# Another step table for the attention stage: value turns, second unit copy and softmax steps placed at other quarters

## The chip, the cores and the metric

The kernel runs on one core of one Trainium2 chip. The metric is the device time of one execution in microseconds (us), lower is better. A core has TensorE (matmuls and transposes, PE in the profile; its weight loads are PEld), VectorE (DVE), ScalarE (ACT), GpSimd (POOL) and SyncE (SP), which here only issues DMAs. Each engine runs its own instructions in program order; they wait for one another by semaphores.

## The reference, cut to what matters

```python
def _L0_attn_ref(x, Wq, bq, Wk, bk, Wv, bv, Wo, bo):      # x: layer-normed, (4, 512, 1024)
    q = (x @ Wq.T + bq).reshape(B, S, H, D)               # H = 32 heads, D = 32
    k = (x @ Wk.T + bk).reshape(B, S, H, D)
    v = (x @ Wv.T + bv).reshape(B, S, H, D)
    scores = jnp.einsum('bshd,bsgd->bshg', q, k) * inv_sqrt_d     # per token: heads against heads
    scores = jnp.where(scores > THRESH, scores, -jnp.inf)
    attn = jax.nn.softmax(scores, axis=-1)
    out = jnp.einsum('bshg,bsgd->bshd', attn, v).reshape(B, S, Hd)
    return out @ Wo.T + bo

xn = _layernorm(x)
out = x + _L0_attn_ref(xn, ...) + _L0_ffn_ref(xn, ...)    # ffn: int4 weights with group scales, silu(gate) * up, down
```

The attention is over the 32 heads of one token, not over tokens, so each token's scores are a 32 x 32 matrix.

## The kernel before, in words

The 2048 tokens are 16 tiles of 128. The first part of the program turns and splits the weights and projects tile 0. Then `tile_2(i)` is run for i = 1 to 16 (13 of these passes, i = 2 to 14, are a hardware loop). After that come the rest of the output projection and the feed-forward part, 28 tiles of the inner dimension, which the change does not touch.

One pass of `tile_2(i)` has 24 quarters (s = 0 to 23). In each quarter TensorE issues six 128x512 matmuls of the projection of tile i (`project`, L499); four quarters make one "unit", 512 of the 3072 columns of Q, K and V. Units 0 and 1 are Q, 2 and 3 are K, 4 and 5 are V. Behind the matmuls of a quarter stand the steps that the table `STEPS` lists for it. The last pass, i = 16, has no projection: there the quarters hold the turning of Wo (`wo_part`, L567 on TensorE) and the output projection (L586).

The names in `STEPS`, and what each engine does for one:

- **S0 to S3**: scores of the tile before, j = i - 1 (TensorE L529); ScalarE copies them out (L784, four instructions a step).
- **X**: the layer-normed tile i + 1 is split into two f16 parts, ScalarE L756 and VectorE L975.
- **T4 to T7**: the values of tile j, as f16 parts in `stacks`, are turned by TensorE (L513), eight 128x128 transposes a batch. ScalarE copies the even batches to `turned` (L774), VectorE the odd ones (L999). **R0 to R3** are the same for the queries of tile i. Batches use two banks in turn, so a batch waits until the one two before it is copied out (`batch_out`).
- **V0 to V3**: probabilities times values (TensorE L546), copied out by ScalarE (L807) and VectorE (L1028).

Beside the table, at s % 4 == 3, a finished unit is copied: VectorE adds the bias (`unit_copy`, L992), ScalarE makes the two high f16 parts (`unit_part`, L768), GpSimd the two low ones (L1174). R0 waits for the low parts of unit 1. The bank of a unit is free for the next but one when VectorE has copied it.

The softmax of tile j is placed by constants: `SHIFT_AT` (VectorE: row maximum L1006, subtraction L1010), `EXP_AT` (ScalarE: an activation table load and the exponential, L790), `MASK_AT` (VectorE: threshold mask L1014, row sum L1017), `DIVIDE_AT` (VectorE: reciprocal L1021, division L1023), and `P_AT`, where ScalarE writes the high parts of the probabilities (`prob_hi`, L798, eight instructions, the first waits for `norm_done`, the division) and GpSimd the low ones (L1174). SyncE turns them by DMA; V0 waits for the first of four such transposes. SyncE also turns the keys of tile i by DMA; the next pass's S0 waits for it.

In one quarter VectorE does the unit copy first, then the steps of the table, then the softmax piece; ScalarE does the steps of the table, then the softmax piece, then the unit part. So the table and the constants fix the order on each engine:

```python
STEPS = [["S0"], ["S1"], ["S2"], ["S3"], ["X", "T4"], ["T5"], ["T6"], ["T7"], [], [], [], [], ["R0"], ["R1"],
         ["R2"], ["R3"], [], ["V0"], ["V1"], ["V2"], ["V3"], [], [], []]
```

Of the kernel before, what the change touches and what calls it, by code (L numbers as in the profile page):

```python
# [41 lines left out]
def build(nc, x_in, Wq, bq, Wk, bk, Wv, bv, Wo, bo, gate_q, gate_s, up_q, up_s, down_q, down_s, out):  # L42
# [26 lines left out]
    with ExitStack() as whole:  # L69
# [144 lines left out]
        def anchor(eng):  # L214
# [10 lines left out]

        STEPS = [["S0"], ["S1"], ["S2"], ["S3"], ["X", "T4"], ["T5"], ["T6"], ["T7"], [], [], [], [], ["R0"], ["R1"],
                 ["R2"], ["R3"], [], ["V0"], ["V1"], ["V2"], ["V3"], [], [], []]
        QUARTERS = len(STEPS)  # L230

        STATS_AT, ROOT_AT, NORM_AT, SHIFT_AT, EXP_AT, MASK_AT, DIVIDE_AT, P_AT = 0, 2, 2, 3, 4, 5, 6, 8

        LAST_UNITS = (QUARTERS - 2) // 2

# [29 lines left out]
        def steps_of(i, s):  # L265

            for name in STEPS[s]:
                kind, n = name[0], int(name[1:] or 0)
# [1233 lines left out]
```

How the kernel before makes its waits and increments, by code:

```python
        def wait_pos(eng, s, value):  # L292
            if not isinstance(value, int) or value > 0:
                eng.wait_ge(s, value)
# [175 lines left out]
        @block.tensor  # L471
        def _(pe):
            mm, turn = nc.tensor.matmul, nc.tensor.transpose
            pe.wait_ge(const_ready, 2)
            def weights(w):
                pe.wait_ge(w_loaded[w % 4], rows_landed(w))
                wait_pos(pe, w_hi, w - 2)
                wait_pos(pe, w_lo, w - 2)
                for k in range(KT):
                    last = turn(weight_pair(w)[:, k * P:(k + 1) * P], w_rows[:, w % 4, k * P:(k + 1) * P],
                                ident32[:])
                last.then_inc(w_turned, 1)
# [2 lines left out]
            def project(i, s):  # L488
                u, ks = s // 4, range(2 * (s % 4), 2 * (s % 4) + 2)
                if s == 0:
                    pe.wait_ge(x_turned, i * 16 + 16)
                if s % 4 == 0:
                    wait_pos(pe, unit_copied, i * 6 + (u - 1))
# [9 lines left out]
            def batch(j, m):  # L505
                mat = batch_matrix(m)
                if m % 4 == 0:
                    pe.wait_ge(unit_lo, j * 6 + (2 * mat + 2))
                wait_pos(pe, batch_out[m % 2], j * 4 + m // 2)
                for n in range(8):
                    last = turn(batch_bank(m)[:, n * P:(n + 1) * P], stacks[:, mat, 8 * (m % 4) + n, :], ident16[:])
                last.then_inc(batch_done, 1)
# [165 lines left out]
            pe.wait_ge(proj_out, 4 * KT)
            pe.wait_ge(ctx_lo, TT * 4)
```

## Time and profile before

| what | value |
|---|---|
| time, median of 3 runs | 2158.32 us (2156.68 to 2159.87) |
| time of the profiled execution | 2158.44 us |
| its span in the trace | 2156.5 us |
| PE busy | 2034.0 us (94%) |
| DVE busy | 1581.5 us (73%) |
| ACT busy | 1253.2 us (58%) |
| POOL busy | 1348.5 us (63%) |

The difference between the execution's own time and its span lies around the span. Busy shares are means over parts of the program with different limits. The attention passes take the stretch from 78 to about 800 us; the feed-forward part, some 1350 us, comes behind them.

### The profile page before, as it was taken

Reading aid. Unit: us, or ns where it says so; the run is one execution under the profiler, and the core shown is the slowest. Engines: PE = TensorE matmul, PEld = TensorE weight load, DVE = VectorE, ACT = ScalarE, POOL = GpSimd, SP = SyncE. Lnnn points to the kernel's source line nnn. Section 1 sums busy time; section 2 is a strip of 40 time slices with the busy share of each in tenths; the row PEclk is TensorE's granted clock in tenths of the full one; section 3 lists DMA queues with packets and bytes.
Section 4 is the critical chain, followed back from the end, with each engine's and each line's share of the span. In section 5 each row is a group of like instructions: output and inputs, shape, how many; then the busy total and the mean of one; then the engine's idle time right before and its main releaser. Section 6 shows DMA issues by size and latency. Waiting matters only on the chain. (4 is left out here: it accounts for less than half of the span.)

```text
span 2156.5 us, 36938 instructions
## 1 busy us (share of the span) xinstructions
PE 2034.0 (94%) x10880; PEld 973.1 (45%) x10880; DVE 1581.5 (73%) x1584; ACT 1253.2 (58%) x2017; POOL 1348.5 (63%) x769
## 2 busy tenths in 40 slices
PE   8899899989999899989999999999999999999996
PEld 5454445544554444424444444444444444444444
DVE  5565656565656420099999999899989998999897
ACT  4577666766676531226566665666566656565653
POOL 1344454445444200018888888888888888888886
PEclk9999999999999999999999999999999999999998
DMA  8354345444533536211122122112211221122118
GB/s 289 86 118 94 88 93 118 90 88 94 120 88 69 147 93 235 59 44 50 49 66 55 49 58 62 51 49 68 59 44 49 68 58 44 49 68 58 44 25 317
DMA packets 330006, 185.97 MB, mean 86 GB/s; under 512 B 269168, under 2 KB 306032, under 8 KB 329968
## 3 DMA queue, kind: packets, MB, share of 16 engines
q1 hardware_dynamic: 329968, 185.46, 33.0%
q8 instruction: 24, 0.39, 0.1%
q14 instruction: 14, 0.11, 0.0%
HBM read 96.29 MB, written 25.17 MB: 56 GB/s over the span
## 5 line engine op out<-in xcount | busy, mean ns | idle before, releaser
L644 PE MATMUL banks<-xt,lower 128*128 128x512 f16 x3584 | 861.7, 379 | 29.9 <-ACT lower L895 16.2
L1212 POOL TENSOR_TENSOR acc<-acc,lower 128x1024 f32<-128x1024 f32 x327 | 772.0, 2366 | 175.2 <-ACT lower L922 175.2
L922 ACT ACTIVATE lower<-banks,down_scale 128x512 f32<-128x512 f32 x654 | 413.8, 683 | 355.2 <-PE banks L669 263.6
L1099 DVE SCALAR_TENSOR_TENSOR lower<-banks,gate_scale,lower 128x1024 f32<-128x1024 f32 x392 | 479.2, 1277 | 146.2 <-PE banks L644 140.3
L644 PEld LDWEIGHTS banks<-xt,lower 128*128 128x128 f16 x3584 | 337.4, 98 | 486.5 <-DVE lower L1099 80.2
L499 PE MATMUL banks<-wt,xt_tile 128*128 128x512 f16 x2304 | 548.5, 383 | 4.2 <-ACT wt L743 2.6
L1099 DVE SCALAR_TENSOR_TENSOR lower<-banks,up_scale,lower 128x1024 f32<-128x1024 f32 x392 | 479.5, 1278 | 51.0 <-PE banks L644 44.9
L1174 POOL TENSOR_TENSOR stacks<-unit,stacks 128x512 f16<-128x512 f32 x192 | 247.0, 1307 | 375.9 <-ACT stacks L768 375.9
L669 PE MATMUL banks<-lower 128*128 (+1 forms) x1792 | 458.6, 380 | 4.6 <-DMA lower<-lower 4.4
L499 PEld LDWEIGHTS banks<-wt,xt_tile 128*128 (+1 forms) x2304 | 216.7, 99 | 220.1 <-issue 9.9
L669 PEld LDWEIGHTS banks<-lower 128*128 (+1 forms) x1792 | 175.4, 98 | 216.9 <-issue 17.1
L1218 POOL TENSOR_TENSOR lower<-lower 128x1024 f32<-128x1024 f32 x54 | 127.5, 2361 | 191.0 <-DVE lower L1099 191.0
L768 ACT ACTIVATE stacks<-unit 128x512 f16<-128x512 f32 x192 | 110.1, 621 | 131.6 <-DVE unit L992 128.8
L586 PE MATMUL banks<-lower 128*128 128x512 f16 x768 | 170.5, 382 | 3.4 <-ACT acc L820 2.6
L1028 DVE TENSOR_TENSOR ctx_parts<-banks,ctx_parts 32x256 f16<-32x256 f32 x256 | 107.4, 420 | 83.8 <-ACT ctx_parts L807 80.7
L1121 DVE SCALAR_TENSOR_TENSOR acc<-banks,down_scale,acc 128x1024 f32<-128x1024 f32 x106 | 135.6, 1279 | 22.3 <-PE banks L669 22.3
L999 DVE COPY turned<-banks 128x1024 f16<-128x1024 f16 x64 | 77.9, 1217 | 64.4 <-PE banks L513 64.4
L513 PE MATMUL banks<-ident,stacks 128*128 128x128 f16 x1024 | 80.3, 223 | 45.4 <-ACT turned L774 27.7
L807 ACT ACTIVATE ctx_parts<-banks 32x256 f16<-32x256 f32 x256 | 96.0, 375 | 45.1 <-PE banks L546 40.9
L1222 POOL TENSOR_TENSOR lower<-lower 128x1024 f32 (+1 forms) x54 | 115.5, 2139 | 2.1 <-ACT lower L909 2.1
L586 PEld LDWEIGHTS banks<-lower 128*128 128x128 f16 x768 | 74.8, 98 | 92.8 <-issue 6.5
L513 PEld LDWEIGHTS banks<-ident,stacks 128*128 128x128 f16 x1024 | 66.3, 100 | 86.9 <-ACT turned L774 34.8
(57 smaller groups left out, 1331.4 us busy)
## 6 DMA issues: line engine op xcount, KB each, us to landing
lower<-in_L_ffn_gate_q_dram SPq DMA_DIRECT2D x28, 512.0 KB, 3.6
lower<-in_L_ffn_up_q_dram SPq DMA_DIRECT2D x28, 512.0 KB, 4.4
lower<-in_L_ffn_down_q_dram SPq DMA_DIRECT2D x28, 512.0 KB, 3.9
x_tile<-in_L_attn_x_dram SPq DMA_DIRECT2D x16, 512.0 KB, 3.6
xt_scratch<-xt_tile SPq DMA_DIRECT2D x16, 512.0 KB, 2.8
ctx_scratch<-ctx_parts SPq DMA_DIRECT2D x64, 128.0 KB, 2.1
lower<-ctx_scratch SPq DMA_DIRECT2D x4, 2048.0 KB, 9.3
xt<-xt_scratch SPq DMA_DIRECT2D x4, 2048.0 KB, 15.6
```

Of the source, the lines that this page charges most:

```text
L499: last = mm(psum[:, u % 2, :], xt_tile[:, :, :].rearrange("p a b -> p (a b)")[:, bass.ds(at, P)], wt[:, u // 2, wp, k, (u % 2) * BANK:(u % ...
L513: last = turn(batch_bank(m)[:, n * P:(n + 1) * P], stacks[:, mat, 8 * (m % 4) + n, :], ident16[:])
L586: last = mm(psum[:, output_bank(n), :], wo_t[:, wp, k, ho * P:(ho + 1) * P], ctx_t[c % 2][:, :, cp, k, :], start=(k == 0 and m == 0), stop ...
L644: last = mm(psum[:, 2 * (slot % 3) + c, :], gu_t[:, mat, g, :], xt[:, (2 * half + c) * CT:(2 * half + c + 1) * CT, part, g, :], start=(par ...
L669: last = mm(psum[:, bank, :], weights[:, bass.ds((t % 2) * (KT * P) + ho * P, P)], h_flat[:, bass.ds(at, BANK)], start=(part == HI), stop= ...
L922: run(down_tmp[:, buffer, c * BANK:(c + 1) * BANK], psum[:, 6 + c, :], ACT.Copy, scale=scale)\
L1099: v.scalar_tensor_tensor(out=acc_of[:, half, :], in0=gu_pair(slot % 3), scalar=scale[:, :, :].rearrange("p t k -> p (t k)")[:, bass.ds(t * ...
L1121: v.scalar_tensor_tensor(out=acc[:, half, ho, :], in0=gu_pair(slot % 3), scalar=down_scale[:, :, :].rearrange("p h t -> p (h t)")[:, bass. ...
L1174: return g.tensor_tensor(dst, src, hi, ALU.subtract)
L1212: g.tensor_tensor(acc[:, half, ho, :], acc[:, half, ho, :], down_tmp[:, buffer, :], ALU.add).then_inc(down_added, 1)
L1218: g.tensor_tensor(h_sb[:, half, :], h_sb[:, half, :], u_acc[:, half, :], ALU.mult).then_inc(h_done, 1)
L1222: g.tensor_tensor(h_part(t, half, LO), h_sb[:, half, :], h_part(t, half, HI), ALU.subtract)\
```

## The change

The table and four of the eight constants are changed; nothing else is.

```diff
-        STEPS = [["S0"], ["S1"], ["S2"], ["S3"], ["X", "T4"], ["T5"], ["T6"], ["T7"], [], [], [], [], ["R0"], ["R1"],
-                 ["R2"], ["R3"], [], ["V0"], ["V1"], ["V2"], ["V3"], [], [], []]
+        STEPS = [["S0"], ["S1"], ["S2"], ["S3"], ["X"], ["T4"], ["T5"], [], ["T6"], [], ["T7"], [], ["R0"], ["R1"],
+                 ["R2"], ["R3"], ["V0"], ["V1"], [], ["V2"], ["V3"], [], [], []]
-        STATS_AT, ROOT_AT, NORM_AT, SHIFT_AT, EXP_AT, MASK_AT, DIVIDE_AT, P_AT = 0, 2, 2, 3, 4, 5, 6, 8
+        STATS_AT, ROOT_AT, NORM_AT, SHIFT_AT, EXP_AT, MASK_AT, DIVIDE_AT, P_AT = 0, 2, 2, 3, 5, 7, 7, 8
```

On ScalarE, in each pass, this is the piece behind the exponential. L774 is the copy of batch T6, L768 the high parts of unit 1, L798 the high parts of the probabilities.

```order
 L790 ACT_TABLE_LOAD
 L790 ACTIVATE p_c<-p_c 128x1024
-L774 ACTIVATE turned<-banks 128x128x8
-L768 ACTIVATE stacks<-unit 128x16x32 x2
+L768 ACTIVATE stacks<-unit 128x16x32 x2
+L774 ACTIVATE turned<-banks 128x128x8
 L798 ACTIVATE p_stack<-p_c 128x8x32 x8
 L768 ACTIVATE stacks<-unit 128x16x32 x2
```

The copy of T6 and the high parts of unit 1 have changed places; both still stand ahead of the probabilities.

On VectorE, in each pass, this is the piece behind the split of the next tile (L975). The first L999 is the copy of T5, the second that of T7; the first L992 of either order is the copy of unit 1.

```order
 L975 TENSOR_TENSOR x_parts<-x_tile,x_parts 128x1024
 L999 COPY turned<-banks 128x128x8
-L1014 SCALAR_TENSOR_TENSOR p_c<-s_c,p_c 128x1024
-L1017 TENSOR_REDUCE sums<-p_c 128x32
-L1021 RECIPROCAL sums<-sums 128x32
-L1023 TENSOR_TENSOR p_c<-p_c,sums 128x1024
-L992 SCALAR_TENSOR_TENSOR unit<-banks,bias_qkv 128x512
+L992 SCALAR_TENSOR_TENSOR unit<-banks,bias_qkv 128x512
+L1014 SCALAR_TENSOR_TENSOR p_c<-s_c,p_c 128x1024
+L1017 TENSOR_REDUCE sums<-p_c 128x32
+L1021 RECIPROCAL sums<-sums 128x32
+L1023 TENSOR_TENSOR p_c<-p_c,sums 128x1024
```

The copy of unit 1 now stands ahead of the mask, the sum, the reciprocal and the division. T7's copy stands behind the division in both orders.

On TensorE, this is the piece from the last score step to R0, first before, then after. L529 is S3, L513 are T4 to T7 and then R0.

```order
L529 MATMUL banks<-turned 128x128 x8
L499 MATMUL banks<-wt,xt_tile 128x512 x6
L513 MATMUL banks<-ident,stacks 128x128 x8
L499 MATMUL banks<-wt,xt_tile 128x512 x6
L513 MATMUL banks<-ident,stacks 128x128 x8
L499 MATMUL banks<-wt,xt_tile 128x512 x6
L513 MATMUL banks<-ident,stacks 128x128 x8
L499 MATMUL banks<-wt,xt_tile 128x512 x6
L513 MATMUL banks<-ident,stacks 128x128 x8
L499 MATMUL banks<-wt,xt_tile 128x512 x30
L513 MATMUL banks<-ident,stacks 128x128 x8
```

```order
L529 MATMUL banks<-turned 128x128 x8
L499 MATMUL banks<-wt,xt_tile 128x512 x12
L513 MATMUL banks<-ident,stacks 128x128 x8
L499 MATMUL banks<-wt,xt_tile 128x512 x6
L513 MATMUL banks<-ident,stacks 128x128 x8
L499 MATMUL banks<-wt,xt_tile 128x512 x12
L513 MATMUL banks<-ident,stacks 128x128 x8
L499 MATMUL banks<-wt,xt_tile 128x512 x12
L513 MATMUL banks<-ident,stacks 128x128 x8
L499 MATMUL banks<-wt,xt_tile 128x512 x12
L513 MATMUL banks<-ident,stacks 128x128 x8
```

T4 and T5 have moved one quarter back, T6 two and T7 three; R0 is where it was. V0 and V1 come one quarter earlier than before, V2 and V3 where they were.

## Rows read from the trace of the kernel before

**Rows 1.** Stretches: passes 2 to 14 of the attention, and pass 15.
```profile
core 0: us, PE busy (x) PEld busy (x) DVE busy (x) ACT busy (x) POOL busy (x), PEclk, DMA share, GB/s
119.66:679.53 559.87, 513.78 (x3538) 274.61 (x3537) 341.42 (x508) 388.54 (x793) 266.93 (x260) 0.98 0.44 97
679.53:721.47 41.94, 38.92 (x273) 20.83 (x272) 24.24 (x35) 26.29 (x58) 19.58 (x20) 1.00 0.42 96
```

**Rows 2.** Waits of TensorE in passes 2 to 14: total us, times, longest.
```profile
PE banks L513 <- ACT turned L774: 25.6, 13, 2.0
PE banks L513 <- POOL stacks L1174: 11.1, 13, 1.2
PE banks L546 <- DVE ctx_parts L1028: 5.6, 13, 0.4
```

**Rows 3.** Timeline of TensorE, one pass: start, duration, instruction, [idle before].
```profile
293.22 0.61 PE L529 MATMUL banks<-turned 128*128 128x128 f16 x8
293.67 1.46 PE L499 MATMUL banks<-wt,xt_tile 128*128 128x512 f16 x6
294.97 0.61 PE L529 MATMUL banks<-turned 128*128 128x128 f16 x8
...
305.81 0.62 PE L513 MATMUL banks<-ident,stacks 128*128 128x128 f16 x8 [1.97 <-ACT turned L774]
...
308.21 0.62 PE L513 MATMUL banks<-ident,stacks 128*128 128x128 f16 x8 [0.48 <-DVE turned L999]
...
316.55 0.62 PE L513 MATMUL banks<-ident,stacks 128*128 128x128 f16 x8 [1.24 <-POOL stacks L1174]
```

**Rows 4.** Timeline of ScalarE, the same pass.
```profile
308.03 1.01 ACT L774 ACTIVATE turned<-banks 128x1024 f16<-128x1024 f16 x1
312.92 1.15 ACT L768 ACTIVATE stacks<-unit 128x512 f16<-128x512 f32 x2 [3.88 <-DVE unit L992]
313.97 2.54 ACT L798 ACTIVATE p_stack<-p_c 128x256 f16<-128x256 f32 x8
316.42 1.13 ACT L768 ACTIVATE stacks<-unit 128x512 f16<-128x512 f32 x2
317.46 1.00 ACT L774 ACTIVATE turned<-banks 128x1024 f16<-128x1024 f16 x1
```

**Rows 5.** Timeline of VectorE, the same pass.
```profile
292.78 0.69 DVE L992 SCALAR_TENSOR_TENSOR unit<-banks,bias_qkv 128x512 f32<-128x512 f32 x1
...
304.84 2.18 DVE L975 TENSOR_TENSOR x_parts<-x_tile,x_parts 128x1024 f16<-128x1024 f32 x1
306.94 1.21 DVE L999 COPY turned<-banks 128x1024 f16<-128x1024 f16 x1
308.16 1.22 DVE L1014 SCALAR_TENSOR_TENSOR p_c<-s_c,p_c 128x1024 f32<-128x1024 f32 x1
...
311.06 1.22 DVE L1023 TENSOR_TENSOR p_c<-p_c,sums 128x1024 f32<-128x1024 f32 x1
312.20 0.68 DVE L992 SCALAR_TENSOR_TENSOR unit<-banks,bias_qkv 128x512 f32<-128x512 f32 x1
```

**Rows 6.** Timeline of GpSimd, the same pass.
```profile
303.84 4.19 POOL L1174 TENSOR_TENSOR stacks<-unit,stacks 128x512 f16<-128x512 f32 x2 [6.83 <-ACT stacks L768]
...
314.14 2.27 POOL L1174 TENSOR_TENSOR stacks<-unit,stacks 128x512 f16<-128x512 f32 x2 [6.11 <-ACT stacks L768]
```

**Rows 7.** The split of the next tile on VectorE, all 16: min/median/max ns.
```profile
L975 DVE TENSOR_TENSOR x_parts<-x_tile,x_parts x16: 1225/2176/2176, 8.3 to 649.4; 128x1024 f16<-128x1024 f32 x16
```

**Rows 8.** DMA issues in passes 2 to 14: times, us from issue to landing.
```profile
probs_t<-p_stack SPq DMA_TRANSPOSE x52, 3.3
...
turned<-stacks SPq DMA_TRANSPOSE x13, 6.7
```

**Rows 9.** One quarter of TensorE behind the wait for T4's copy, pass 12.
```profile
565.00 2.77 PE L499 MATMUL banks<-wt,xt_tile 128*128 128x512 f16 x6
```

**Rows 10.** The stretch there; columns as in the first group, PEclk is 0.50.
```profile
565.00:567.00 2.00, 2.00 (x7) 0.76 (x6) 2.00 (x3) 1.99 (x3) 1.43 (x1) 0.50 0.00 0
```

## The prediction

> **What bounds the kernel now.** First the windows: passes 2 to 14 take 559.87 us, 43.07 us each, and TensorE is busy in 513.78 of them, ahead of ScalarE (388.54), VectorE (341.42) and GpSimd (266.93) [rows 1]. So TensorE sets the pace, with gaps. Its own time for a pass comes from its timeline: a batch of eight small matmuls takes 0.45 us from start to start and a quarter of the projection 1.30 [rows 3]; 16 x 0.45 + 24 x 1.295 = 38.3 us. The other 4.8 us of each pass are stalls, and the change can win no more than these: 13 x 4.8 = 62 us there. The list of waits names them, the same in all 13 passes [rows 2]: T6 waits for ScalarE's copy of T4, 1.97; R0 for GpSimd's low parts of unit 1, 1.2; V2 for VectorE, 0.4; and T7 sometimes for VectorE's copy of T5, 0.48 [rows 3]. (From start to start the four cost more than the listed idle time, 2.1, 0.65, 1.4 and 0.6; they sum to the 4.8.)
>
> Then the other engines of one pass, to see what makes each late. ScalarE is a chain without a gap from the scores to the copy of T6 at 308.03; then it idles 3.88 us for VectorE's copy of unit 1 [rows 4]. VectorE has no gap from 304.84 to 312.20: split, T5, mask, sum, reciprocal, division, and only then unit 1, which was ready long before [rows 5]. R0 waits behind just this: VectorE 312.20, ScalarE 312.92, GpSimd 314.14 to 316.41, R0 at 316.55 [rows 3 to 6].
>
> **The change part by part**, on the clock of that pass. Nothing up to T4's copy on ScalarE is moved, so that copy still ends near 305.75, the time at which T6 starts now.
>
> *T4 to T7 later on TensorE.* R0 stays behind quarter 12 and no work is added. T6 has two more quarters ahead of it: S0 at 293.22 plus 8 quarters and 6 batches, 293.22 + 10.36 + 2.7 = 306.3, after the copy of T4. The 2.1 us are gone. T7 comes at 309.3, its bank was emptied at 308.15 [rows 5]: the 0.65 is gone. V2 has one more quarter behind V1: the 0.6 is gone.
>
> *Unit 1 ahead of the mask.* VectorE starts it at 308.16 in place of the mask and ends at 308.85; ScalarE's exponential ended at about 308.1, where T6's copy starts now [rows 4], so it takes unit 1 at 308.9 and ends at 310.05; GpSimd works from 310.1 to 312.4. TensorE comes to R0 at 293.22 + 12 x 1.295 + 8 x 0.45 = 312.35. The 1.4 us shrink to some 0.2.
>
> *What is late next.* The mask is pushed back by the unit copy, 0.61: 308.77. The division, 2.90 behind the mask [rows 5], would start at 311.67. But it reads two SBUF tensors while GpSimd is busy. What that costs is shown by the split L975: 1.23 us where GpSimd is idle, 2.18 in the passes [rows 7], where GpSimd's unit 0 takes 4.19 in place of 2.27 [rows 5, 6]. They take turns by instruction. GpSimd's second instruction of unit 1 starts at about 311.25, before the division, so I let the division wait to 312.2 and end at 313.4: +0.55. The Trainium skill says the same in "SBUF — State Buffer", "Who interferes with whom": of a VectorE instruction with two SBUF inputs and a GpSimd instruction that reads SBUF, the one that issues second blocks until the first has finished. By that rule the pass has this 0.55; by a reading in which they share without blocking it has not. The trace agrees with the rule.
>
> ScalarE has copied T6 at 311.0 and then stands at the probabilities, which wait for the division: a new idle time of 2.4 us, with unit 2's parts and R0's copy queued behind it. Eight instructions, 2.45 us to the next, from 313.45 to 315.9; unit 2 to 316.95; R0's copy 1.02, to 317.97 [rows 4]. **R2 needs that copy**, as both use one bank. TensorE would reach R2 without waits at 312.35 + 2 x 1.745 = 315.8. It starts at 318.0. On the way R1 waits some 0.3 for T7's copy on VectorE (313.3 to 314.5), which is part of these 2.2 us, as is R0's 0.2. So three waits of 3.35 us and a fourth of 1.4 become R0 0.2, R1 0.3, R2 1.7.
>
> *The rest of the pass* has no wait. V0, one quarter earlier, comes at 318.0 + 0.45 + 1.3 + 0.45 + 1.3 = 321.5. The first probabilities leave ScalarE at 314.1, GpSimd at 315.5, and are turned 3.3 us later [rows 8], 318.8: 2.7 us to spare. The next pass starts from VectorE's copy of unit 5, at 292.78 here [rows 5], behind V3's output; V3 keeps its quarter, so this stays within 0.2 us of its place.
>
> A pass is then 38.3 + 2.2 = 40.5, less the 0.1 to 0.2 by which unit 5's copy comes earlier without V2's stall behind it: 40.3 to 40.4. That is **2.7 us less than 43.07**, 35 us for the 13 passes. Pass 1 starts with less queued on ScalarE; I give it 2.4. Pass 15 has no split and no norm: 41.94 [rows 1] becomes its own 38.3 and the 1.5 or so ahead of the Wo turning, 2.2 less. In the last pass the four softmax instructions, 4.04 us from start to start (308.16 to 312.20 [rows 5]), stand in one block on VectorE between two Wo parts, where they stood in two pieces, and TensorE turns Wo one by one behind these: between 0 and 4 us lost, I take 1.5. Sum: 35 + 2.4 + 2.2 - 1.5 = 38 us. Against the profiled execution's 2158.4 us, practically the median of 2158.3, that is 2120.4. Nothing behind pass 16 is touched; its length is taken as it is.
>
> **The clock** is the one large unknown. In the windows the mean granted clock of the 13 passes is 0.98 [rows 1]. It is half (1.2 GHz for 2.4) for short stretches behind the 1.97 us wait: a quarter of 1.46 us took 2.77 there [rows 9, 10]. 2% of 560 us is 11 us of TensorE time lost over the passes. Now it costs nothing, since the waits of T7 and R0 come behind it and shrink by as much. After the change the long wait is R2's, 1.7 us, and behind it the pass has no wait left: the same falls would cost their full 11 us, and more if they came in each pass (1.3 x 13 = 17). The wait is shorter than the one that the clock fell behind, and TensorE's timeline shows no fall behind R0's 1.24. So the likeliest is that little of it comes: I add 1 us. **2121 us.** The Trainium skill ("TensorE: Matmul & The Clock Gate", "A second HAM failure mode: psum-queue depth-cycling") lets the clock swing where TensorE idles briefly between groups of matmuls; by it the time would be that of the second case below.
>
> **The rivals.**
> - *As forecast*, 0.64: 2115 to 2126 by the errors of the hand-built pass (0.3 us of each of 15).
> - *The clock falls behind R2's wait*, 0.17: the same relief, less 7 to 17 us: 2127 to 2138. For it: 11 us over 13 passes, at 1.3 us or more a fall, mean that it followed the wait of T6 often. Against: R2's wait is shorter than that one by 0.3 to 0.4 us.
> - *The division isn't held*, 0.08: it starts before GpSimd's second instruction, or does not block. 0.55 x 14 = 8 us more: 2112.
> - *VectorE is held more often*, 0.06: if the mask or the sum are also pushed behind GpSimd's unit 1, the block is another 1 to 2 us late, and with it the probabilities, R0's copy and R2: 20 us less gain, 2141. Against: by the list above the mask has ended (310.0) when GpSimd starts.
> - *Slower*, 0.03: V0 a quarter earlier meets probabilities that are not yet turned. Its slack is 2.7 us; it eats the gain of 2.7 when the turning takes 3.3 + 2.7 + 2.7 = 8.7 us, more than the keys' whole transpose (6.7 [rows 8]). At 9.7 us a pass loses 1 us: 2173.
> - *No effect*, 0.02: ScalarE's chain is the true limit and R2's wait grows to all of the 4.8 us: 2158. It would need the division 2.6 us later than worked out.
>
> **How the numbers follow.** The predicted time is the first case's. The range 2112 to 2133 takes in the third case and the lower half of the second, some 0.8 in all. What a measurement of this kernel can tell from no change is about 0.2%, 4.3 us. Faster holds but for the last two: 0.95; within 0.2% 0.02, slower 0.03.
>
> **What would show it.** The changed kernel's list of waits should have no wait of T6 or T7 and none of V2; a wait of L513 for ScalarE's L774 of about 1.7 us in each pass, now for R0's copy; ScalarE idle some 2.4 us ahead of L798, for VectorE's L1023; L1023 at 1.7 to 1.8 us in place of 1.22; passes of 40.4 us. Passes that differ by 1 us or more, with a clock under 1.00, would show the second case; L1023 at 1.22 and passes under 40 the third; a wait of L546 for the DMA `probs_t`, the fifth. The prediction is wrong if a wait that the list of before does not name, as of S0 for the turned keys, stands in the new one.

## The result, and the profile after

The changed kernel takes 2120.85 us, the median of four runs (2118.47 to 2122.11), against 2158.22 us before. The ratio is 0.982, with a 95% interval of 0.981 to 0.984: 37 us less. The prediction said 2121, 2112 to 2133. Its profiled execution took 2121.04 us with a span of 2119.1 us. (The change touches three of the eight constants, `EXP_AT`, `MASK_AT` and `DIVIDE_AT`, and not four, as the text on the change has it.)

First the stretches, as in [rows 1]: passes 2 to 14, pass 15, and from the first Wo turning to the first matmul of the feed-forward part.

```profile
core 0: us, PE busy (x) PEld busy (x) DVE busy (x) ACT busy (x) POOL busy (x), PEclk, DMA share, GB/s
119.18:642.09 522.91, 501.61 (x3538) 273.92 (x3537) 347.91 (x508) 389.56 (x793) 267.37 (x260) 1.00 0.47 103
642.09:680.49 38.40, 37.11 (x268) 20.59 (x266) 23.25 (x33) 26.36 (x58) 19.63 (x20) 1.00 0.42 95
680.49:874.16 193.67, 181.99 (x928) 87.65 (x928) 26.25 (x40) 50.51 (x95) 7.32 (x10) 0.99 0.41 133
```

These windows begin at S0; those of [rows 1] begin a quarter earlier. From S0 to the first Wo turning, pass 15 took 40.65 us in the kernel before, and from there to the feed-forward part it was 190.95. The feed-forward part itself takes 1244 us in both kernels; the 1350 us given ahead of the prediction have the rest of the output projection in them.

The 13 passes take 40.22 us each in place of 43.07, and the mean clock in them is 1.00 in place of 0.98. Then the list of TensorE's waits in these 13 passes, which answers to [rows 2]. It is one line long:

```profile
PE banks L513 <- ACT turned L774: 20.4, 13, 1.6
```

TensorE's timeline of one pass tells which wait this is. Its rows are, in order, T6, T7, R0, R1, R2 and V2:

```profile
293.12 0.61 PE L513 MATMUL banks<-ident,stacks 128*128 128x128 f16 x8
...
296.16 0.61 PE L513 MATMUL banks<-ident,stacks 128*128 128x128 f16 x8
...
299.20 0.61 PE L513 MATMUL banks<-ident,stacks 128*128 128x128 f16 x8
...
301.17 0.62 PE L513 MATMUL banks<-ident,stacks 128*128 128x128 f16 x8
...
304.65 0.62 PE L513 MATMUL banks<-ident,stacks 128*128 128x128 f16 x8 [1.57 <-ACT turned L774]
...
312.93 0.61 PE L546 MATMUL banks<-probs_t,turned 128*128 128x128 f16 x8
```

T6, T7, R0 and V2 wait for nothing. R2 waits 1.57 us. R1 stands 1.97 us behind R0, where 1.75 is the pace of a step without a wait ([rows 3]: S0 at 293.22, S1 at 294.97), so it lost 0.2.

On ScalarE the same pass shows where R2's wait comes from. The rows are unit 1, T6's copy, the probabilities, unit 2 and R0's copy:

```profile
295.40 1.15 ACT L768 ACTIVATE stacks<-unit 128x512 f16<-128x512 f32 x2 [0.66 <-DVE unit L992]
296.45 1.00 ACT L774 ACTIVATE turned<-banks 128x1024 f16<-128x1024 f16 x1
300.09 2.56 ACT L798 ACTIVATE p_stack<-p_c 128x256 f16<-128x256 f32 x8 [2.63 <-DVE p_c L1023]
302.56 1.13 ACT L768 ACTIVATE stacks<-unit 128x512 f16<-128x512 f32 x2
303.60 1.00 ACT L774 ACTIVATE turned<-banks 128x1024 f16<-128x1024 f16 x1
```

ScalarE stands 2.63 us in front of the probabilities for the division, and R0's copy ends at 304.60, right before R2 at 304.65. In [rows 4] its idle time stood in front of unit 1's parts, and the probabilities came right behind them without a wait. VectorE's rows are unit 1, mask, division and T7's copy; GpSimd's row below them is unit 1:

```profile
294.69 0.68 DVE L992 SCALAR_TENSOR_TENSOR unit<-banks,bias_qkv 128x512 f32<-128x512 f32 x1
295.29 1.21 DVE L1014 SCALAR_TENSOR_TENSOR p_c<-s_c,p_c 128x1024 f32<-128x1024 f32 x1
...
298.17 1.80 DVE L1023 TENSOR_TENSOR p_c<-p_c,sums 128x1024 f32<-128x1024 f32 x1
299.90 1.21 DVE L999 COPY turned<-banks 128x1024 f16<-128x1024 f16 x1
```

```profile
296.63 2.27 POOL L1174 TENSOR_TENSOR stacks<-unit,stacks 128x512 f16<-128x512 f32 x2 [1.97 <-ACT stacks L768]
```

The division takes 1.80 us where it took 1.22 [rows 5]. GpSimd's second instruction runs from 297.74 to 298.90. The division starts beside it, at 298.17, and ends at 299.98, 1.08 us behind its end.

### The profile page after: what moved, and what is told of

It reads as the page before. It is cut to its first block and busy times, and to the rows that moved or that the text cites. A ratio compares the mean times of both kernels' runs of the same rounds, so it can differ in the third digit from the quotient of the medians.

```text
span 2119.1 us, 36938 instructions
## 1 busy us (share of the span) xinstructions
PE 2021.6 (95%) x10880; PEld 973.3 (46%) x10880; DVE 1589.2 (75%) x1584; ACT 1253.2 (59%) x2017; POOL 1348.6 (64%) x769
## 5 line engine op out<-in xcount | busy, mean ns | idle before, releaser
L499 PE MATMUL banks<-wt,xt_tile 128*128 128x512 f16 x2304 | 542.0, 380 | 4.2 <-ACT wt L743 2.6
L768 ACT ACTIVATE stacks<-unit 128x512 f16<-128x512 f32 x192 | 110.2, 621 | 79.8 <-DVE unit L992 79.3
L1174 POOL TENSOR_TENSOR p_stack<-p_c,p_stack 128x256 f16<-128x256 f32 x128 | 81.1, 670 | 63.3 <-ACT p_stack L798 63.3
L1222 POOL TENSOR_TENSOR lower<-lower 128x1024 f32 (+1 forms) x54 | 115.4, 2137 | 2.1 <-ACT lower L909 2.1
L992 DVE SCALAR_TENSOR_TENSOR unit<-banks,bias_qkv 128x512 f32<-128x512 f32 x96 | 65.7, 685 | 60.3 <-PE banks L499 59.4
L784 ACT ACTIVATE s_c<-banks 32x256 f32<-32x256 f32 x256 | 95.8, 374 | 11.9 <-PE banks L529 8.2
```

The source lines that it names most:

```text
L499: last = mm(psum[:, u % 2, :], xt_tile[:, :, :].rearrange("p a b -> p (a b)")[:, bass.ds(at, P)], wt[:, u // 2, wp, k, (u % 2) * BANK:(u % ...
L768: last = run(dst[n], src, ACT.Copy)
L1174: return g.tensor_tensor(dst, src, hi, ALU.subtract)
L1222: g.tensor_tensor(h_part(t, half, LO), h_sb[:, half, :], h_part(t, half, HI), ALU.subtract)\
```

## The experiments

Ten kernels were run. Ratios are to the kernel before on the same chip; the changed kernel's is 0.982. "A pass" is the distance from S0 to S0 in the profiled execution. All of them change only the table and the constants, and the diffs are against the changed kernel unless it says otherwise.

### The parts of the change by themselves

The table without the unit copy:

```diff
-STATS_AT, ROOT_AT, NORM_AT, SHIFT_AT, EXP_AT, MASK_AT, DIVIDE_AT, P_AT = 0, 2, 2, 3, 5, 7, 7, 8
+STATS_AT, ROOT_AT, NORM_AT, SHIFT_AT, EXP_AT, MASK_AT, DIVIDE_AT, P_AT = 0, 2, 2, 3, 5, 6, 6, 8
```

> The new table of steps and the exponential at quarter 5, but mask, sum, reciprocal and division stay ahead of unit 1's copy on VectorE, as before the change. Theory: T6, T7 and V2 find their banks free, so their three waits (3.35 us a pass) go, but TensorE then only arrives earlier at what unit 1 holds up: R0 waits some 2.3 us and the first quarter of unit 3 (quarter 12, which needs unit 1's bank) another 1.8 us. A pass is 42.3 us in place of 43.07, the time 2158 less 8, about 2150. Rival: the two parts of the change win their own waits each; then this one alone saves 13 x 3.35 = 43 us, 2115.

Measured: 2168.78 us, ratio 1.005 (1.003 to 1.007), slower than the kernel before. TensorE's waits are the two that were expected, a little shorter (2.14 and 1.51 us for 2.3 and 1.8; the first line counts passes 1 and 15, too):

```profile
PE banks L513 <- POOL stacks L1174: 30.9, 15, 2.1
PE banks L499 <- DVE unit L992: 19.6, 13, 1.5
```

The passes are of two lengths: 42.2 us, as expected, in four of the 13, and 43.9 in the other nine. TensorE's timeline of a long one:

```profile
314.56 1.47 PE L499 MATMUL banks<-wt,xt_tile 128*128 128x512 f16 x6 [1.51 <-DVE unit L992]
318.17 0.62 PE L513 MATMUL banks<-ident,stacks 128*128 128x128 f16 x8 [2.14 <-POOL stacks L1174]
318.62 2.06 PE L499 MATMUL banks<-wt,xt_tile 128*128 128x512 f16 x6
320.47 1.06 PE L513 MATMUL banks<-ident,stacks 128*128 128x128 f16 x8
321.32 2.17 PE L499 MATMUL banks<-wt,xt_tile 128*128 128x512 f16 x6
```

Behind the two waits a quarter takes 2.06 and 2.17 us in place of 1.46, and a batch 1.06 in place of 0.61. The granted clock was half there (0.50 in the first row below), and the window over the 13 passes has a mean of 0.97:

```profile
320.00:322.00 2.00, 2.00 (x12) 1.31 (x11) 0.34 (x1) 0.99 (x2) 2.00 (x4) 0.50 0.69 130
121.15:685.05 563.90, 516.60 (x3537) 280.45 (x3536) 342.01 (x508) 388.43 (x793) 266.87 (x260) 0.97 0.44 96
```

My 2150 left this out: 9 falls at 1.68 us are 15 of the 19 us missed. The rival, each part winning its own waits, would have been 2115 and is out. Without the unit copy TensorE only arrives earlier at what unit 1 holds up.

The unit copy without the table (diff against the kernel before):

```diff
-STATS_AT, ROOT_AT, NORM_AT, SHIFT_AT, EXP_AT, MASK_AT, DIVIDE_AT, P_AT = 0, 2, 2, 3, 4, 5, 6, 8
+STATS_AT, ROOT_AT, NORM_AT, SHIFT_AT, EXP_AT, MASK_AT, DIVIDE_AT, P_AT = 0, 2, 2, 3, 4, 7, 7, 8
```

> The old table of steps; mask and division at quarter 7 behind unit 1's copy (T7's copy, which is in the same quarter of the old table, comes ahead of them too). Theory: R0's wait goes, but the division is later and ScalarE stands at the probabilities, so R2 waits some 1.2 us instead; the waits of T6, T7 and V2 stay. A pass is 42.8 us, the time 2156 to 2157. Rival: R0's wait of 1.4 us is won in each of 15 passes, 2137.

Measured: 2156.37 us, ratio 0.9995 (0.9985 to 1.0004), no difference, and the rival's 2137 is out. But the time is right for a partly wrong reason. The shortest passes are 42.14 us and R2's wait in them is 0.32, not the 42.8 and 1.2 that I wrote; the other seven are 43.0 to 43.8. In each of the seven the clock falls behind T6's wait of 1.97, and R0 no longer waits behind it to take it up. In five of them the mask then runs beside GpSimd's unit 1 and is held, as the division is in the changed kernel:

```profile
348.68 2.20 DVE L1014 SCALAR_TENSOR_TENSOR p_c<-s_c,p_c 128x1024 f32<-128x1024 f32 x1
```

That is the mechanism of the prediction's fourth case (VectorE is held more often). In the changed kernel the mask ends at 296.50 and GpSimd starts at 296.63, so only 0.13 us kept it away.

The two parts alone give +10 us (with V0 and V1 moved, too) and -2 us, and together -37.

The other two kernels move only V0 and V1. First the changed kernel with the old places:

```diff
-["R2"], ["R3"], ["V0"], ["V1"], [], ["V2"], ["V3"], [], [], []]
+["R2"], ["R3"], [], ["V0"], ["V1"], ["V2"], ["V3"], [], [], []]
```

> The changed kernel with V0 and V1 back at quarters 17 and 18. Theory: V2 follows V1 by one quarter again and waits 0.6 us for VectorE, and the outputs of V0 to V3 come later on ScalarE and VectorE, so the copy of unit 5 and with it the next pass's scores start later: a pass of 41.0 us, 11 us over the changed kernel, 2132. Rival: only V2's stall comes back, and R2's wait absorbs it since ScalarE's chain is the limit: 2121 to 2123.

Measured: 2131.55 us, ratio 0.988 (0.986 to 0.989), 41.07 us a pass. V2 waits again, and R2's wait has not absorbed it:

```profile
PE banks L513 <- ACT turned L774: 20.4, 13, 1.6
PE banks L546 <- DVE ctx_parts L1028: 5.6, 13, 0.4
PE banks L513 <- DVE turned L999: 2.9, 13, 0.2
```

Then the kernel before with the new places (the same two lines, the other way round):

> The kernel before with only V0 and V1 moved one quarter earlier. Theory: V2's stall goes and the copy of unit 5 comes earlier, 42.3 us a pass, 2147. Rival: the stalls of T6, T7 and R0 grow by what V2's loses: 2158.

Measured: 2147.52 us, ratio 0.995 (0.993 to 0.997), 42.2 us a pass. This part is worth 11 us whichever way it is tried. The rest of the gain, some 27 us, needs the other two parts together: the kernel with the table alone already has V0 and V1 in their new places and is slower than the kernel before all the same.

### R2's wait, and what holds the division

R2 one quarter later, in front of R3:

```diff
-["R2"], ["R3"], ["V0"], ["V1"], [], ["V2"], ["V3"], [], [], []]
+[], ["R2", "R3"], ["V0"], ["V1"], [], ["V2"], ["V3"], [], [], []]
```

> The changed kernel with only R2 moved from quarter 14 to 15, behind which R3 stays. Theory: the one long wait left (1.57 us in each pass, R2 for ScalarE's copy of R0, which stands behind the probabilities) is covered by one more quarter of 1.3 us; what is left of it is some 0.2 us. A pass is 38.9 to 39.0 us in place of 40.22, the time 2121 less 18, 2103. Rival: ScalarE and VectorE are a closed loop as long as the pass, so the wait comes back elsewhere (S2, V0) and the time stays at 2118 to 2121.

Measured: 2102.71 us, ratio 0.974 (0.973 to 0.976), 38.94 us a pass. What is left of the wait over the 13 passes:

```profile
PE banks L513 <- ACT turned L774: 3.6, 13, 0.3
```

So the wait was a step standing ahead of its data by about one quarter, and not a loop of ScalarE and VectorE as long as the pass.

The division behind T7's copy:

```diff
-STATS_AT, ROOT_AT, NORM_AT, SHIFT_AT, EXP_AT, MASK_AT, DIVIDE_AT, P_AT = 0, 2, 2, 3, 5, 7, 7, 8
+STATS_AT, ROOT_AT, NORM_AT, SHIFT_AT, EXP_AT, MASK_AT, DIVIDE_AT, P_AT = 0, 2, 2, 3, 5, 7, 10, 10
```

> The changed kernel with reciprocal, division and the probabilities at quarter 10: on VectorE the division now stands behind T7's copy, when GpSimd has ended unit 1. Theory: the division takes 1.22 us in place of 1.80 since nothing of GpSimd's runs beside it, and R1's short wait goes, but it ends 0.7 us later and R2's wait grows to 2.3 us or more: 41.0 us a pass. With the clock at full that is 2134; a wait over 1.97 us has been followed by half clock elsewhere, and nothing covers it here, so 1.7 us more in up to 13 passes: 2134 to 2156, 2148 if two passes in three. Rival 1: the division's 1.80 us is its own (a cost of its place in the order), then it stays 1.80. Rival 2: the clock has nothing to do with the waits, then all passes are 41.0 and the time 2134.

Measured: 2136.87 us, ratio 0.990 (0.989 to 0.992). The division in this kernel, and under it in the changed one (min/median/max ns):

```profile
L1023 DVE TENSOR_TENSOR p_c<-p_c,sums x16: 1224/1225/1226, 98.5 to 737.1; 128x1024 f32<-128x1024 f32 x16
```

```profile
L1023 DVE TENSOR_TENSOR p_c<-p_c,sums x16: 1227/1805/1809, 97.1 to 713.2; 128x1024 f32<-128x1024 f32 x16
```

1225 against 1805 ns: the 0.58 us are GpSimd's, not the division's own. The 1227 of the changed kernel is from the last pass, in which GpSimd has no unit. In the kernel with the table alone, where GpSimd starts unit 1 behind the division, all 16 take 1224 or 1225 ns. R2's wait is 2.23 us here (2.3 said). Ten of the 13 passes are 40.64 us, not 41.0, and three are 42.26, with a fall of the clock behind R2's wait:

```profile
349.85 1.03 PE L513 MATMUL banks<-ident,stacks 128*128 128x128 f16 x8 [2.23 <-ACT turned L774]
```

I had expected two in three. The rival that the clock has nothing to do with the waits (all passes alike) is out as well, though its 2134 was nearer than my 2148.

R0 one quarter earlier:

```diff
-STEPS = [["S0"], ["S1"], ["S2"], ["S3"], ["X"], ["T4"], ["T5"], [], ["T6"], [], ["T7"], [], ["R0"], ["R1"],
+STEPS = [["S0"], ["S1"], ["S2"], ["S3"], ["X"], ["T4"], ["T5"], [], ["T6"], [], ["T7"], ["R0"], [], ["R1"],
```

> The changed kernel with only R0 moved from quarter 12 to 11. Theory: R0 then waits 1.2 to 1.3 us for GpSimd's low parts of unit 1, in place of R2's 1.57; R1 and R2 have one more quarter behind it and find their copies done. A pass is 39.5 us, the time 2111. Rival: R2 waits on ScalarE's probabilities whatever R0 does, and R0's new wait comes on top: 2121 or more.

Measured: 2108.5 us, ratio 0.978 (0.976 to 0.979), 39.37 us a pass. R0 now waits for GpSimd, a little less than I said, and R1 and R2 wait for nothing:

```profile
PE banks L513 <- POOL stacks L1174: 12.5, 13, 1.0
```

The probabilities at quarter 12, behind R0's copy:

```diff
-STATS_AT, ROOT_AT, NORM_AT, SHIFT_AT, EXP_AT, MASK_AT, DIVIDE_AT, P_AT = 0, 2, 2, 3, 5, 7, 7, 8
+STATS_AT, ROOT_AT, NORM_AT, SHIFT_AT, EXP_AT, MASK_AT, DIVIDE_AT, P_AT = 0, 2, 2, 3, 5, 7, 7, 12
```

> The changed kernel with the probabilities at quarter 12, behind unit 2 and the copy of R0 on ScalarE. Theory: R0's copy no longer stands behind the wait for the division, so R2's wait falls from 1.57 to about 1 us (VectorE's copy of unit 2 still stands behind the division), but the probabilities come 3.5 us later and V0 now waits some 2.6 us for their turning by DMA: a pass of 42.3 us, and 2149 with the clock at full. Rival (a time that ScalarE's order sets as a whole): the passes stay near 40.2, 2121.

Measured: 2164.96 us, ratio 1.003 (1.002 to 1.004). Both waits have about the expected size (the first line counts one of pass 1, too):

```profile
PE banks L546 <- DMA probs_t<-p_stack: 35.8, 14, 2.6
PE banks L513 <- ACT turned L774: 11.1, 13, 0.9
```

And the clock falls again behind the long one, here shown at V0 and V1:

```profile
281.24 0.61 PE L546 MATMUL banks<-probs_t,turned 128*128 128x128 f16 x8 [2.56 <-DMA probs_t<-p_stack]
283.98 1.06 PE L546 MATMUL banks<-probs_t,turned 128*128 128x128 f16 x8
```

Three passes are 42.25 us, the forecast, and ten are 43.9. 10 x 1.65 = 16 us is all that was missed (2165 against 2149). So a V0 that comes ahead of its probabilities, the mechanism of the prediction's slower rival, does cost this much. In the changed kernel the first of them had landed 2.5 us before V0 came (2.7 said).

### The last pass, and all steps moved

```diff
-STATS_AT, ROOT_AT, NORM_AT, SHIFT_AT, EXP_AT, MASK_AT, DIVIDE_AT, P_AT = 0, 2, 2, 3, 5, 7, 7, 8
+STATS_AT, ROOT_AT, NORM_AT, SHIFT_AT, EXP_AT, MASK_AT, DIVIDE_AT, P_AT = 0, 2, 2, 3, 5, 7, 7, 9
```

> The changed kernel with the probabilities at quarter 9 in place of 8. In passes 1 to 15 nothing stands between, so no engine's order changes there; in the last pass ScalarE turns one more Wo part ahead of them. Theory: of the 2.7 us that the last pass and what follows it (first Wo turn to first feed-forward matmul, 193.67 us against 190.95 before) lost, the wait of 1.82 us for a Wo part stems from ScalarE's eight probability instructions, 2.45 us, standing ahead of that part; it goes or falls under 0.8, the stretch is some 1 us shorter, the passes stay at 40.22, the time 2120. Rival (the prediction's own step): it is the block of four softmax instructions on VectorE, which stays; then the wait stays at 1.8.

Measured: 2119.66 us, ratio 0.982 (0.980 to 0.984); the difference to the changed kernel is inside the noise, so only the trace can tell. The first line is the wait of 1.82 us in the changed kernel, the second what stands in its place:

```profile
720.50 0.63 PE L567 MATMUL banks<-ident,lower 128*128 128x128 f32 x4 [1.82 <-DVE lower L1034]
722.45 0.63 PE L567 MATMUL banks<-ident,lower 128*128 128x128 f32 x4 [0.45 <-DVE lower L1034]
```

The block on VectorE was not moved. So that wait was ScalarE's, whose probabilities stood ahead of the Wo part.

The stretch from the first Wo turning to the feed-forward part is 192.27 us in place of 193.67, but not all of these 1.40 us are the probabilities'. Half lies ahead of them, in the first output matmul's wait. Here it is in the changed kernel, then in this one (where the list names VectorE, whose row ends 0.02 us behind the landing of the load):

```profile
687.99 4.33 PE L586 MATMUL banks<-lower 128*128 128x512 f16 x12 [2.21 <-DMA lower<-ctx_scratch]
687.14 4.44 PE L586 MATMUL banks<-lower 128*128 128x512 f16 x12 [1.48 <-DVE lower L1034]
```

The load of the context was issued at the same place in both (3.4 us ahead of the first Wo turning) and landed 0.73 us earlier here, by chance or for a reason that these runs don't show. From the first output matmul to the feed-forward part it is 185.50 us in place of 186.17 (184.87 in the kernel before). So the place of the probabilities is worth 0.67 us.

The last kernel gives each step its quarter by when its bank is free:

```diff
-STEPS = [["S0"], ["S1"], ["S2"], ["S3"], ["X"], ["T4"], ["T5"], [], ["T6"], [], ["T7"], [], ["R0"], ["R1"],
-         ["R2"], ["R3"], ["V0"], ["V1"], [], ["V2"], ["V3"], [], [], []]
-STATS_AT, ROOT_AT, NORM_AT, SHIFT_AT, EXP_AT, MASK_AT, DIVIDE_AT, P_AT = 0, 2, 2, 3, 5, 7, 7, 8
+STEPS = [["S0"], ["S1"], ["S2"], ["S3"], [], ["T4"], ["X"], ["T5"], [], ["T6"], [], ["T7"], ["R0"], [],
+         ["R1"], [], ["R2", "R3", "V0"], ["V1"], [], ["V2"], ["V3"], [], [], []]
+STATS_AT, ROOT_AT, NORM_AT, SHIFT_AT, EXP_AT, MASK_AT, DIVIDE_AT, P_AT = 0, 2, 2, 5, 6, 8, 8, 10
```

> A table worked out from the rows so that no step comes before its bank is free: X at 6, T4 5, T5 7, T6 9, T7 11, R0 12, R1 14, R2 and R3 16, V0 16, V1 17, the row maximum at 5, the exponential at 6, mask and division at 8, the probabilities at 10. Theory: no wait over 0.1 us is left in passes 1 to 15, each is TensorE's own 38.3 us, the Wo pass is some 4 us shorter than the changed kernel's: 2121 less 13 x 1.95, less 4, 2091. Rival: with ScalarE and VectorE pushed back, the next pass's start (unit 5's copy, the turned keys) becomes the limit: 39.5 us a pass or more, 2110.

Measured: 2089.21 us, ratio 0.968 (0.967 to 0.970), the fastest of all: 69 us under the kernel before. Passes 2 to 14:

```profile
116.87:614.59 497.72, 497.22 (x3537) 276.05 (x3536) 335.14 (x508) 385.79 (x793) 273.61 (x260) 1.00 0.50 109
```

TensorE is busy in 497.22 of 497.72 us. Twelve of the 13 passes are 38.23 us, with no wait listed, and one is 38.9 (one wait of 0.5 for a turning DMA). That is the 38.3 that the prediction worked out as TensorE's own. The Wo stretch is 188.98 us, 4.7 less than the changed kernel's (some 4 said).

## Why the prediction was right

**What can be won.** The own time of a pass was put at 38.3 us and the stalls at 4.8; the kernel with all steps moved runs at 38.23. One reading was too even: the four waits are not the same in all 13 passes. In eight they are as listed; in the five in which the clock fell behind T6's wait, T7 waits for nothing and R0 0.2 us, and the pass is 43.07 us all the same.

**The three waits that go.** T6, T7 and V2 wait for nothing, as said. V2's part was tried alone both ways and is 11 us of the 37.

**Unit 1 ahead of the mask.** R0 waits for nothing where I left 0.2.

**What is late next.** ScalarE's new idle time is 2.63 us (2.4 forecast) in front of the probabilities, the division is 1.80 us (1.22 + 0.55 forecast). From start to start R2 is 1.73 us late (1.7; its listed idle time is 1.57) and R1 0.2 (0.3). A pass is 40.22 us against 40.3 to 40.4, for want of R0's 0.2. Moving R2 by one quarter took 1.28 us of a pass, almost a whole quarter of 1.30, which shows that this wait, and nothing behind it, was the limit of the changed kernel. That the division is held by GpSimd was a step taken from the split's 2.18 us [rows 7]. It is now shown for the division itself, by the kernel in which it has no neighbour and takes 1.225. The Trainium skill's rule ("SBUF — State Buffer", "Who interferes with whom"), that of two such instructions the one that issues second blocks until the first has finished, fits all of these.

**The sum.** From S0 to S0, pass 1 is 2.44 us shorter (2.4 said), passes 2 to 14 are 36.96 (35), pass 15 to the first Wo turning 2.25 (2.2). The stretch from there to the feed-forward part is 2.72 us longer (193.67 against 190.95), where I took 1.5. The start of the program and the feed-forward part, which the change doesn't touch, are together 1.5 us longer in this execution; the four runs of the changed kernel lie 3.6 us apart. 36.96 + 2.44 + 2.25 - 2.72 - 1.5 = 37.4. The terms are right, but that the time agrees within 0.2 us is luck: the 13 passes gave 2 us more than forecast, the last pass 1.2 less, the 1.5 are chance, and the 1 us added for the clock wasn't needed.

**The term with the wrong mechanism** is the last pass, "the four softmax instructions ... in one block on VectorE". Its size was within my 0 to 4 us, its place was not. The block cost nothing: behind it TensorE turned the next Wo part without a wait, while in the kernel before a wait of 0.77 us had stood behind the first of the two pieces. Of the 2.72 us, 1.30 lie behind the first output matmul (186.17 us against 184.87). About half of these, 0.67, are the probabilities on ScalarE, as the kernel with these at quarter 9 showed. Another wait there, for the Wo part behind the row maximum and the subtraction, grew from 1.34 to 1.78 us; T4's batch used to stand in front of it. The other 1.42 us are the first output matmul's wait for the context loaded by DMA, 2.21 us in place of 0.79. That load stands behind the turning of the keys on SyncE and was issued 3.4 us ahead of the first Wo turning, where before it was 4.2. Both were read from the traces only, not tried, and the load that landed 0.73 us sooner in the kernel with the probabilities at 9 shows that its issue does not explain all.

**The clock** took none of the gain: no fall behind R2's 1.57 us in the 13 passes, and the mean clock is 1.00. The likeliest case held, and so far as the runs go its reason (a shorter wait than the one it fell behind): the kernel before with the new places of V0 and V1 has a wait of T6 of 1.73 us, and no fall in 13 passes either. The price of the other case was set somewhat high. The trace of the kernel before has five falls in its 13 passes, and at 1.6 to 1.7 us a fall, as the experiments have it, that is 8 us, not the 11 read from a mean rounded to 0.98. The case itself is real: with waits of 2.1 to 2.6 us it came in three of the experiments and cost 1.6 to 1.7 us a fall. With the division behind T7's copy it is R2's own wait, longer by 0.66 us, that brings it.

## What to carry to other kernels

Where one engine is the pace and the others feed it through a few banks, lay its steps out by when each bank is really free, read from the slower engines' rows; a step one quarter too early can cost a whole quarter in every pass (R2: 1.28 us of 1.30), and the table alone or the reordering alone may lose (+10 us) or win next to nothing (-2). After taking a wait away, walk along the in-order queues to the next instruction that stands in front of its data (here the probabilities, with R0's copy behind them), and price that one before trusting the sum. Don't count a wait by its length alone: behind waits of 1.97 to 2.6 us TensorE came back at half clock in three to ten of 13 passes, and what that costs depends on whether another wait stands behind it to take it up.

## What the runs showed of the hardware

The granted clock after a wait of TensorE was not the same from pass to pass of one execution. Counted in passes 2 to 14 of one profiled execution each:

| wait of TensorE in each pass, us | kernel | passes with half clock behind it |
|---|---|---|
| 1.57 | changed; V0 and V1 at their old places; probabilities at 9 | 0 of 13 in each |
| 1.73 | before, V0 and V1 moved | 0 of 13 |
| 1.97 | before | 5 of 13 |
| 1.97 | unit copy alone | 7 of 13 |
| 2.14, with one of 1.51 shortly ahead | table alone | 9 of 13 |
| 2.23 | division behind T7's copy | 3 of 13 |
| 2.56, with one of 0.85 ahead | probabilities at 12 | 10 of 13 |

A pass with a fall was 1.6 to 1.7 us longer where no wait stood behind it, 0.9 to 1.7 in the kernel with the unit copy alone, and no longer at all in the kernel before, where T7's and R0's waits shrank by as much. What decides between the passes of one kernel these runs don't tell.

An instruction of VectorE with two SBUF inputs waited only for the instruction of GpSimd that was then running, and ended 1.08 us behind it, wherever in that instruction it started. The division was 1.80 us where GpSimd's second had begun 0.43 us ahead of it, 1.53 where it had begun 0.70 ahead (unit copy alone), and 1.22 where GpSimd had nothing to do. It works both ways: beside the split of the next tile, a GpSimd instruction of 1.16 us took 2.1.
